# A decoder layer on one core: attention's x turned by a DMA of 16-bit planes, keys scaled first, scores scaled in four operations, residual behind the gate product

## The reference

```python
x = x + mamba(_layernorm(x), W_in, conv_w, conv_b, dt_bias, A_log, D_param, norm_w, W_out)   # state space block
x = x + xattn(_layernorm(x), ctx_2048, mask, Wq, bq, Wk, bk, Wv, bv, Wo, qn_w, kn_w)          # 16 heads, 4 key/value heads
x = x + ffn(_layernorm(x), w_gate, w_up, w_down, ln_weight)                                   # int8 activations, ternary weights
```

## Time and profile before

| | |
|---|---|
| time, median of 3 runs | 1190.26 us (1189.74 to 1191.51) |
| the profiled execution | 1191.23 us |
| its span, first to last instruction | 1189.5 us |
| mean granted clock of PE | 0.983 |
| PE busy | 1119.2 us, 94% |
| DVE busy | 1005.5 us, 85% |
| POOL busy | 935.8 us, 79% |
| ACT busy | 819.7 us, 69% |
| DMA queue of SP | 45.75 MB, 14.8% of 16 engines |

### The profile page before, as it was taken

One profiled execution on the slowest core, in us unless ns is written; L12 is line 12 of the kernel. 1 busy time (PEld: TensorE's weight loads), 2 busy tenths in 40 slices (PEclk: granted clock), 3 DMA queues, 4 the chain that ended last, 5 costly groups with the idle time before them and its releaser, 6 DMA issues.

```text
span 1189.5 us, 34826 instructions
## 1 busy us (share of the span) xinstructions
PE 1119.2 (94%) x11405; PEld 983.7 (83%) x11405; DVE 1005.5 (85%) x2509; ACT 819.7 (69%) x2066; POOL 935.8 (79%) x1514
## 2 busy tenths in 40 slices
PE   4889999999999999999999999999999999999964
PEld 3678888898888889888888988888898888888753
DVE  4766898898889889888988988898898889888666
ACT  4586777677667767766776776677677667766641
POOL 4788788888888888888888888888888888878651
PEclk8899999999999999999999999999999999999987
DMA  8311101111110111111011111101111110121000
GB/s 297 87 50 24 33 17 31 37 37 35 33 37 15 29 37 37 35 33 37 15 29 37 37 35 33 37 15 29 37 37 35 33 37 15 29 35 30 22 9 23
DMA packets 103306, 46.31 MB, mean 39 GB/s; under 512 B 80352, under 2 KB 101600, under 8 KB 103008
## 3 DMA queue, kind: packets, MB, share of 16 engines
q1 hardware_dynamic: 100336, 45.75, 14.8%
q10 hardware_dynamic: 2928, 0.03, 0.1%
HBM read 23.93 MB, written 4.19 MB: 24 GB/s over the span
## 4 chain that ended last, share of the span: by engine, by line
PE 66%; DVE 13%; ACT 13%; issue 4%; POOL 2%; DMA 1%; ACTq 1%; POOLq 0%; DVEq 0%; SPq 0%
PE bank L1800 18%; PE bank L1882 5%; PE bank L1860 5%; PE bank L1718 4%; PE bank L1690 4%; PE bank L1691 4%; PE bank L1692 4%; DVE hh L1389 3%; DVE hh L1382 3%; ACT kb L875 3%; PE bank L1813 3%; PE bank L1940 2%; PE bank L1707 2%; PE bank L1870 2%; PE bank L1762 2%
## 5 line engine op out<-in xcount | busy, mean ns | idle before, releaser
L1800 PE MATMUL bank<-xcT,wq 128*128 128x128 f32 x2048 | 234.1, 275 | 2.2 <-ACT xcT L862 2.2
L1800 PEld LDWEIGHTS bank<-xcT,wq 128*128 128x128 f32 x2048 | 231.2, 192 | 2.9 <-issue 2.5
L1223 DVE SCALAR_TENSOR_TENSOR xc<-bank,cw,xc 128x124 f32<-128x124 f32 (+2 forms) x576 | 163.7, 339 | 11.6 <-ACT xc L831 3.0
L1690 PE MATMUL bank<-wo_hi,o_hi 128*128 128x256 f32 x512 | 149.5, 292 | 1.1 <-DVE o_lo L1312 1.1
L1691 PE MATMUL bank<-wo_lo,o_hi 128*128 128x256 f32 x512 | 143.7, 281 | 0.0
L1692 PE MATMUL bank<-wo_hi,o_lo 128*128 128x256 f32 x512 | 143.3, 280 | 0.0
L887 ACT ACTIVATE qT<-bank,bqT 128x128 f32<-128x128 f32 x384 | 109.6, 372 | 41.0 <-PE bank L1800 41.0
L530 POOL TENSOR_TENSOR pr<-pr,mask 128x512 f32<-128x512 f32 x64 | 79.9, 1270 | 38.1 <-DVE pr L1331 38.0
L1690 PEld LDWEIGHTS bank<-wo_hi,o_hi 128*128 128x128 f32 x512 | 96.4, 188 | 1.5 <-DVE o_lo L1312 1.4
L1691 PEld LDWEIGHTS bank<-wo_lo,o_hi 128*128 128x128 f32 x512 | 96.7, 189 | 0.1
L1692 PEld LDWEIGHTS bank<-wo_hi,o_lo 128*128 128x128 f32 x512 | 96.5, 188 | 0.0
(11 more groups left out here) (239 smaller groups left out, 3414.5 us busy)
## 6 DMA issues: line engine op xcount, KB each, us to landing
x_in<-in_x SPq DMA_DIRECT2D x32, 128.0 KB, 2.1
c_in<-in_ctx SPq DMA_DIRECT2D x32, 128.0 KB, 2.1
x_m<-in_x SPq DMA_DIRECT2D x32, 128.0 KB, 2.2
out<-x SPq DMA_DIRECT2D x32, 128.0 KB, 1.7
wq<-in_L_xattn_Wq SPq DMA_DIRECT2D x1, 2048.0 KB, 14.1
stage<-in_L_xattn_Wo SPq DMA_DIRECT2D x2, 1024.0 KB, 8.4
w_in<-in_L_attn_W_in SPq DMA_DIRECT2D x1, 1024.0 KB, 6.3
qT<-in_L_ffn_w_gate SPq DMA_DIRECT2D x1, 1024.0 KB, 12.9
```

The source lines that it names most:

```text
L1223: last = v.scalar_tensor_tensor(out=o, in0=src, scalar=cw[:, j, TAPS - 1 - back:TAPS - back], in1=o, op0=ALU.mult, op1=ALU.add)
L1690: mm(out, left[0], right[0], start=first, stop=False)
L1800: last = mm(x_Qbank[g][:, (n % 4) * P:(n % 4 + 1) * P], wq[:, c, n * HD:(n + 1) * HD], xcT[:, c, :], start=(c == 0), stop=(c == DC - 1))
```

## The change

Six edits, in the hunks below:

1. x of attention is turned by a DMA from tile 4 on: ACT splits x_xn into two 16-bit planes (`x_split_halves`), SP issues `turn_x`, ACT joins them into xcT (`x_join_halves`). PE's `x_transpose` and ACT's `x_T_copy` remain for the first four tiles. The planes lie in the second half of the same part of q2 that holds the context's. On SP, turn_x stands behind turn_f, and turn_c goes ahead of turn_m.
2. For this the norm of x is applied earlier: on DVE ahead of the convolution of B and C, on POOL ahead of `f_rms`.
3. On ACT the keys are scaled directly behind `f_keep`, and the tanh of z goes ahead of the taps and the splits. `x_keep` and `x_hold` go ahead of `c_join_halves`.
4. The scores are scaled in four DVE operations of 256 columns in place of two of 512, and the first mask on POOL waits for the third of them alone.
5. On DVE `f_residual` moves from behind the query bias to behind the gate product.
6. PE's third group of queries, which writes the bank of the turned keys, now waits itself for kT's copy.

```diff
-        M_TURN, C_TURN = 4, 2
+        x_halves = c_flat[:, 2 * D:3 * D].bitcast(U16)
+        x_halvesT = c_flat[:, 3 * D:4 * D].bitcast(U16).rearrange("p (g n) -> p g n", g=2 * DC)
+        M_TURN, C_TURN, X_TURN = 4, 2, 4
...
+            def turn_x(t):
+                count(sp, s["x_planes"], t - X_TURN + 1)
+                sp.sem_inc(s["sp_waited"].sem, 1)
+                count(sp, s["x_turned"], (t - X_TURN) * 16)
+                sp.sem_inc(s["sp_waited"].sem, 1)
+                sp.dma_start_transpose(x_halvesT, x_halves).then_inc(s["x_turned"].sem, 16)
...
                     turn_f(i - 3)
+                if not isinstance(i, int) or X_TURN <= i < TILES:
+                    turn_x(i)
+                if not isinstance(i, int) or C_TURN <= i < TILES:
+                    turn_c(i)
                 if not isinstance(i, int) or M_TURN <= i + 2 < TILES:
                     turn_m(i + 2)
-                if not isinstance(i, int) or C_TURN <= i < TILES:
-                    turn_c(i)
...
             def x_mask(t, n):
-                after(pool, x_s1[1], t + 1)
+                after(pool, (x_sa, x_s1)[n][1], t + 1)
...
                     x_khat(xa)
+                if m is not None:
+                    x_norm(m)
                 if f is not None:
                     f_rms(f)
-                if m is not None:
-                    x_norm(m)
...
+            def x_split_halves(t):
+                after(act, s["x_xn"], t + 1)
+                count(act, s["x_turned"], (t - X_TURN) * 16)
+                sc.copy(x_halves.rearrange("p (g n) -> p g n", g=2),
+                        x_xn[:].bitcast(U16).rearrange("p (n g) -> p g n", g=2)).then_inc(s["x_planes"].sem, 1)
+
+            def x_join_halves(t):
+                count(act, s["x_turned"], (t - X_TURN + 1) * 16)
+                after(act, x_Q[3], t)
+                after(act, s["x_TT"], t)
+                sc.copy(xcT[:, 0:DC, :].rearrange("p c n -> p (c n)").bitcast(U16).rearrange("p (n g) -> p g n", g=2),
+                        x_halvesT.rearrange("p (g c) n -> p g (c n)", g=2)).then_inc(s["x_TT"].sem, 1)
...
-                if xa is not None:
+                if xa is not None and isinstance(xa, int) and xa < X_TURN:
                     x_T_copy(xa)
...
                     f_keep(f)
+                if xa is not None:
+                    x_khat(xa)
                 if mn is not None:
+                    m_tanh_z(mn)
                     m_tap_bc(mn)
+                if m is not None and (not isinstance(m, int) or m >= X_TURN):
+                    x_split_halves(m)
                 if m is not None:
                     c_split_halves(m)
                 if ms is not None:
                     m_split_halves(ms)
                 if mn is not None:
-                    m_tanh_z(mn)
-                if xa is not None:
-                    x_khat(xa)
-                if mn is not None:
                     m_tanh_bc(mn)
                 if xa is not None:
                     x_kT_copy(xa)
+                if m is not None and (not isinstance(m, int) or m >= X_TURN):
+                    x_join_halves(m)
+                if xa is not None:
+                    x_keep(xa)
+                if m is not None:
+                    x_hold(m)
                 if m is not None:
                     c_join_halves(m)
-                if xa is not None:
-                    x_keep(xa)
-                if m is not None:
-                    x_hold(m)
...
             def x_norm(t):
-                after(dve, s["x_T"], t)
+                if isinstance(t, int) and t <= X_TURN:
+                    after(dve, s["x_T"], t)
+                else:
+                    count(dve, s["x_planes"], t - X_TURN)
...
-                v.tensor_tensor(pr[:, :, a, :], (X0, X1)[a][:, :].rearrange("p (j e) -> p j e", j=NPAIR),
-                                bcast(rq[:, 1, a * NPAIR:(a + 1) * NPAIR].unsqueeze(2), [P, NPAIR, SEQ]),
-                                ALU.mult).then_inc(x_s1[a].sem, 1)
+                for n in range(2):
+                    pairs = slice(4 * n, 4 * n + 4)
+                    v.tensor_tensor(pr[:, pairs, a, :], (X0, X1)[a][:, 256 * n:256 * n + 256].rearrange("p (j e) -> p j e", j=4),
+                                    bcast(rq[:, 1, a * NPAIR + 4 * n:a * NPAIR + 4 * n + 4].unsqueeze(2), [P, 4, SEQ]),
+                                    ALU.mult).then_inc((x_sa, x_s1)[n][a].sem, 1)
...
-                if fb is not None:
-                    f_residual(fb)
...
                     m_gate(m)
+                if fb is not None:
+                    f_residual(fb)
...
                     m_silu_z(mn)
+                if m is not None:
+                    x_norm(m)
+                if mn is not None:
                     m_conv_bc(mn)
...
                     m_silu_bc(mn)
-                if m is not None:
-                    x_norm(m)
...
                     after(pe, s["x_scaled1"], t)
+                elif g == 2:
+                    after(pe, s["x_kT"], t)
...
-                if xa is not None:
+                if xa is not None and isinstance(xa, int) and xa < X_TURN:
                     x_transpose(xa)
```

More of the change, by code:

```diff
@@ L220, in decoder_layer @@
           m_tap m_convb+m_conva m_tb+m_ta m_bc+m_xs m_G m_Gm+m_Ma m_Xtr m_Xdt m_xd
-          m_Y m_y+m_yf m_sq m_ssy m_v4+m_ry m_out m_x1 m_planes m_turned c_planes c_turned c_xT f_qturned
+          m_Y m_y+m_yf m_sq m_ssy m_v4+m_ry m_out m_x1 m_planes m_turned c_planes c_turned c_xT f_qturned x_planes x_turned
           x_hold x_copy x_stats+x_mean x_veps+x_rstd x_xn x_T x_TT x_K+x_V x_kb+x_vb x_ksq x_kv+x_rk+x_kh
           x_chi+x_clo x_KT x_kT x_Q0+x_Q1+x_Q2+x_Q3 x_qb1 x_qb0+x_qb2+x_qb3 x_sq0+x_sq1+x_sq2+x_sq3 x_ss x_ssc x_ssT x_qv x_rq
-          x_S0+x_S1 x_scaled0+x_scaled1 x_masked0+x_masked1 x_mx0+x_mx1 x_less0+x_less1 x_ex0+x_ex1
+          x_S0+x_S1 x_part0+x_scaled0+x_part1+x_scaled1 x_masked0+x_masked1 x_mx0+x_mx1 x_less0+x_less1 x_ex0+x_ex1
           x_sum0+x_inv0+x_sum1+x_inv1 x_p0+x_p1 x_PT0+x_PT1 x_pT0+x_pT1 x_O0+x_O1
@@ L238, in decoder_layer @@
         x_q2 = [s["x_sq0"], s["x_sq1"], s["x_sq2"], s["x_sq3"]]
+        x_sa = [s["x_part0"], s["x_part1"]]
         x_S, x_s1, x_s2 = [s["x_S0"], s["x_S1"]], [s["x_scaled0"], s["x_scaled1"]], [s["x_masked0"], s["x_masked1"]]
@@ L1147, in body @@
                     x_kT_copy(xa)
-                if m is not None:
-                    c_join_halves(m)
+                if m is not None and (not isinstance(m, int) or m >= X_TURN):
+                    x_join_halves(m)
                 if xa is not None:
@@ L1153, in body @@
                     x_hold(m)
+                if m is not None:
+                    c_join_halves(m)
             act.wait_ge(s["c_round"].sem, 1)
```

## The result

The changed kernel takes 1273.47 us (median of 4 runs, 1272.83 to 1273.85) against 1190.88 us of the kernel before measured beside it: a ratio of 1.0693, 95% interval 1.0675 to 1.0712. The forecast was 1248 with a range of 1222 to 1274, and slower; the time lies 25 us above the forecast and 0.5 us inside the upper end. The profiled execution has a span of 1271.0 us against 1189.5.

What follows compares the result with a forecast made beforehand. PE's order was taken as the loop's clock, busy 34.19 of 34.70 us. f's transfer +60, h's transfer +21, keys -17 and transposes -6 made +58: 1249 us by the profiled run, 1248 by the median, range 1222 to 1274.

Steps and rivals of the forecast that it cites:

- Part 4: Residual behind the gate product on DVE: the store then delays f's transfer on SP, stalling PE 2.1 us; +60 us.
- Part 2: x turned by a transfer: PE gains 0.22 us, but SP's queue delays h's transfer, a 0.8 us stall; +21 us.
- Rival A: SP's queue: f's transfer costs 2.1 us, h's transfer nothing; 1227 us, chance 0.20.
- Rival B: Transfers land late beside loads and the store, h 0.9 and f 0.2 us more; 1277 us, chance 0.13.
- part 1: Keys scaled first on ACT: the keys' turn on PE starts 0.59 us earlier each iteration; -17 us.
- Part 3: Scores scaled in four DVE operations: at most 0.5 us more, hidden in DVE's idle time; 0 on PE.
- Rival D: DVE also becomes the bound through x_in's late load, 0.3 us more per iteration; 1256 us, within the forecast's 0.58 chance.
- the 6 of the transposes: PE loses x's two transposes, 0.22 us in each of 28 iterations; -6 us.

Runs made afterwards that it cites:

- e2: The changed kernel with SP issuing f's transfer ahead of the store, the residual staying behind the gate product: 1200.42 us, ratio 1.0077 to the kernel before.
- e3: The kernel before with only the residual moved behind the gate product: 1272.14 us, ratio 1.0689.
- e6: e2 with x also put behind c and m on ACT and in SP's queue: 1183.06 us, ratio 0.994 to the kernel before.
- e10: e2 with x_residual also moved ahead of the last operation of f_hquant on DVE: 1200.75 us, ratio 1.0085 to the kernel before.
- e7: e6 with x_residual also moved ahead of the last operation of f_hquant on DVE: 1179.40 us, ratio 0.9905 to the kernel before.
- e5: The kernel before with only ACT's order changed, keys scaled directly behind f_keep and tanh of z ahead of the taps: 1175.89 us, ratio 0.9873.
- e8: The kernel before with only the scores scaled in four operations, the first mask waiting for the third: 1191.31 us, ratio 1.0001.
- e1: The changed kernel with the residual put back ahead of the average on DVE: 1199.47 us, ratio 1.0069 to the kernel before.
- e12: e7 with m_spread on DVE also moved behind the softmax's sums: 1177.81 us, ratio 0.9898 to the kernel before.
- e4: The changed kernel with the residual one operation earlier, between m_skip and the gate product: 1230.54 us, ratio 1.0324 to the kernel before.

## Why the prediction was right, and where it fell short

**Part 4, f's transfer: right in mechanism and place, 0.3 us short in size.** e2 and e3 show it from both sides: the order on SP alone takes the wait away, and the residual's place alone makes it. I compare the steps from the down product before them, 597.74 in the forecast's frame (632.44 less 34.70) and 596.87 in the changed kernel. The store is issued 15.95 us behind it (612.82) in place of 15.81, as the mixing and with it the gate product come a little later. The store still follows the residual by 0.40 us, as forecast. The gap between the store and the next issue was taken as 0.2 us and is 0.40 (613.17 to 613.57): I took the lower value, that of two transfers in a row, where the row of two loads in the loop gave 0.39. From f's issue to PE's first weight load it is 2.42 us in place of 2.49. Together 0.27 us more. From the down product to the output projection PE takes 22.48 us (634.16 to 656.64, the steady 37.29 less 14.81) against 20.10 before: 2.38 in place of 2.1, 28 x 0.28 = 8 us. The bounds of this term were added up wrongly: by its own numbers they are 1.9 and 2.7 us, not 2.0 and 2.6. The measured value lies within either.

**The granted clock: the term that wasn't in the sum.** Before, the loop ran at 1.00, the 2.4 GHz level, throughout. Now PE stands idle 2.2 us before L1954 (2.4 to 2.6 as listed), and in 6 of the 28 iterations (four in the loop, and iterations 4 and 31) the clock falls there (in 31 with a wait of only 1.6 us by the weight load, and one of 0.7 us shortly ahead of it): 0.55 over 2.9 us, which is nearly all at the 1.2 GHz level. Such an iteration of the loop is 1.3 to 1.5 us longer (38.60, 38.68, 38.71, 38.78 against 37.3): some 8 us in all. In e3 it's 9 of the loop. The forecast named no price for the clock, though the stall that it worked out was the first of its length in the loop. The Trainium skill (TensorE: Matmul & The Clock Gate, HAM oscillation — how this bites in real kernels) says that waits for DMA between groups of products can throttle the clock again and again, and the traces here agree, for some of the waits.

**Part 2, h's transfer: right.** The forecast had the down product 14.60 us behind the output projection, as before, with all gains of PE eaten up. It is 14.81 (619.35 to 634.16). Counted as in the forecast, the stall is 0.81 + 0.21 = 1.0 us in place of 0.8; the trace lists 0.55 of it before L1976, and 0.36 lie in the longer scores (below). SP's gaps are 1.51, 1.38 and 1.50 us in place of 1.39 each; 26 x 0.21 = 5 us. e6 shows that the queue is the cause, and not h's data or its flight, since the same data sent 1.0 us earlier removes the wait. Rival A, which had h's wait at nothing, is out; so, for these transfers, is what the Trainium skill (DMA: Bandwidth & Descriptors, Issuing engines are not separate DMA queues) says of the issue being usually small: each issue ahead of h holds it back by 1.38 to 1.51 us. Rival B, late landings, isn't what brought the time near its 1277: h's landing is 2.7 us by the median, and f's 2.4.

**A wait that the forecast overlooked, and that cost nothing.** The second half of the scores waits for x_residual on DVE (X1 is its bank), 0.36 us an iteration: the scores take 2.45 instead of 2.08 us. It should have stood in the list of deliveries of part 1. e10 shows that it is free as long as h's transfer ends later; e7, where taking it away gains 3.7 us, that it isn't quite free after that. With it in the sum, the forecast would have been the same.

**Part 1: right.** The scalings end at 624.16, 1.5 us ahead of the keys' turn at 625.70, as forecast; alone they are worth 15 us (e5), of the 17 that were worked out. In the changed kernel these, and the 6 of the transposes, are in h's wait, by the place of the down product; no run shows it by taking them out.

**Part 3: right**, nothing (e8).

**Rival D: it happened, at a third of its size.** The forecast had DVE's lateness reach PE at the turn of x and cost 0.3 us. The turn of x keeps its place (9.37 us behind the down product, 9.36 before), but the mixing starts 12.17 us behind the down product by the median of 18 iterations of the loop, 12.07 before, and PE is listed 11 times as waiting for DVE's xdt there. It is 12.17 in e1 as well, where part 4 is undone, so PE's other stalls don't hide it. The gate product, the residual and the store wait for the mixing, so this 0.1 us is part of the 2.38. e12, from e7, shows the cause, the very load of x_in that the forecast named: with that wait out of DVE's way the mixing starts at 11.99.

**The sum as measured:** 28 x 2.38 = 67, 26 x 0.21 = 5 and 6 x 1.4 = 8, together 80, the 80.0 us between the output projections. The forecast had 60 and 21 - 23 = -2, which makes 58. This sum takes the steady iteration's values for all; single intervals near the end differ from them, with 0.66 us more from iteration 29 to 30 and 4.09 from 30 to 31.

**What was luck.** The change costs 83 us and the forecast said 58. Of the 25 missing, f's transfer has 8, the clock 8, and h's transfer with what it eats up 7; the rest lies outside the 28 intervals. The upper end of the range came from rival B, whose late landings didn't occur, and nothing in the range stood for the clock. That the two waits come, where they come and that they cost some 60 us was worked out; that the time still ended 0.5 us inside the range was luck.

## What to carry to other kernels

An operation's place on its engine also decides when the waits that it releases let other queues go on. Before moving one, follow its semaphore to the in-order queue that waits for it, and list all that stands behind that wait: here a residual moved by 7 us on an engine with time to spare cost 80 us by itself (e3), because a store waited for it in front of a transfer that PE needed.

Where several transfers leave one queue, the one with its data last belongs last, unless it's wanted first; and as long as one delivery sets the time, savings ahead of it are worth nothing (e10). Part 1 gains 15 us alone, and by the place of the down product nothing behind a late transfer.

## What the runs showed of the hardware that was not expected

- Waits of PE of 2.2 us in each iteration, at otherwise full work, brought the granted clock down in 4 of the loop's 25 iterations in one kernel and in 9 of 25 in another (e3), though by the weight loads all waits of these two loops lie between 2.20 and 2.25 us; waits of 1.0 us in the loop never did (e4). A fall cost 1.3 to 1.5 us. What decides which of the waits it is stays open.
- On SP the next transfer in the loop is issued 0.19 us after the end of the issue before it for some pairs (c and m), 0.31 to 0.32 for others (x and c, m and h), and 0.40 behind a store.
